# Self-attention's first norm and first projections moved into the adapter's slots

## What is computed

```python
# adapter, L0
hs = _mha(hidden_states @ Wq, enc @ Wk, enc @ Wv)                 # 8 heads of 20
ca_hs1 = _mha(ca_q1[:, indices, :], residual, residual)           # tokens over x
ca_hs2 = _mha(ca_hs1 @ Wq, ca @ Wk_ca, ca @ Wv_ca)                # 4 token keys
x = (hs + ca_hs2) @ Wout + b_out + residual
# block, L1
y = layer_norm(x, g1, be1)
x = cross_attention(y, y, wq1, wk1, wv1, wo1, bo1) + x            # 20 heads of 64
```

## Time and profile before

| | us |
|---|---|
| median of 3 runs | 1039.35 |
| lowest and highest run | 1038.76, 1040.11 |
| the profiled execution | 1038.5 |
| its span | 1036.7 |
| TensorE busy | 981.3 |
| VectorE busy | 690.3 |
| ScalarE busy | 591.5 |
| GpSimd busy | 380.1 |

### The profile page before, as it was taken

How to read it: one execution, slowest core, us unless ns; L and a number is a source line. 1 busy time by engine, 2 the same in 40 slices (tenths; PEclk the granted TensorE clock), 3 DMA queues, 4 the chain that set the end, 5 groups by cost and what they waited for, 6 DMA issues and landing times.

```text
span 1036.7 us, 17534 instructions
## 1 busy us (share of the span) xinstructions
PE 981.3 (95%) x6376; PEld 707.1 (68%) x6376; DVE 690.3 (67%) x1171; ACT 591.5 (57%) x1332; POOL 380.1 (37%) x493
## 2 busy tenths in 40 slices
PE   7999978999999999999999999999989999999998
PEld 4566666666667656667666667666647589999887
DVE  2767646677773776773676773776753889999563
ACT  2666634766763667763667763667753555455442
POOL 2576623434332344342344341343330024444220
PEclk9999999999999999999999999999999999999999
DMA  6400050000000000000000000000000340000000
GB/s 134 94 2 1 1 147 1 1 1 2 1 1 2 1 1 2 1 1 1 2 1 1 1 1 1 2 1 1 2 1 8 101 110 1 1 1 1 2 26 26
DMA packets 25370, 17.64 MB, mean 17 GB/s; under 512 B 8565, under 2 KB 24101, under 8 KB 25285
## 3 DMA queue, kind: packets, MB, share of 16 engines
q1 hardware_dynamic: 25285, 16.52, 6.6%
HBM read 11.26 MB, written 1.31 MB: 12 GB/s over the span
## 4 chain that ended last, share of the span: by engine, by line
PE 64%; DVE 10%; ACT 5%; issue 4%; POOL 1%; DMA 0%; SPq 0%; DVEq 0%; ACTq 0%; POOLq 0%
PE banks L409 13%; PE banks L396 12%; PE banks L382 11%; PE banks L416 4%; ACT sa_probs L499 3%; PE banks L224 3%; PE banks L227 2%; PE banks L226 2%; PE banks L225 2%; PE banks L1641 2%; PE banks L1933 2%; DVE sa_negmax L571 2%; DVE ca_top L1776 2%; DVE ca_probs L1781 1%; PE banks L232 1%
## 5 line engine op out<-in xcount | busy, mean ns | idle before, releaser
L639 POOL TENSOR_SCALAR sa_probs<-sa_probs,sa_inverse 128x512 f32<-128x512 f32 x320 | 217.7, 696 | 372.4 <-DVE sa_inverse L575 372.3
L499 ACT ACTIVATE sa_probs<-banks,sa_negmax 128x512 f32<-128x512 f32 x320 | 215.8, 685 | 163.5 <-DVE sa_negmax L571 163.4
L571 DVE TENSOR_REDUCE sa_negmax<-banks 128x2 f32<-128x1024 f32 x160 | 188.8, 1219 | 12.4 <-PE banks L382 9.7
L396 PEld LDWEIGHTS banks<-ident,sa_probs 128*128 128x128 f32 x1280 | 145.7, 141 | 55.6 <-issue 27.6
L396 PE MATMUL banks<-ident,sa_probs 128*128 128x128 f32 x1280 | 174.0, 277 | 10.0 <-ACT sa_turned L510 5.8
L580 DVE COPY sa_turned<-banks 128x512 f32<-128x512 f32 x160 | 110.2, 689 | 76.3 <-PE banks L396 76.3
L409 PE MATMUL banks<-sa_turned,sa_v 128*64 128x512 f32 x640 | 155.0, 605 | 0.0
L382 PE MATMUL banks<-sa_k_parts,sa_q_parts 64*128 64x512 f32 x960 | 134.9, 412 | 1.9 <-ACT sa_probs L499 1.9
L510 ACT COPY sa_turned<-banks 128x512 f32<-128x512 f32 x160 | 94.3, 590 | 30.6 <-PE banks L396 28.8
L382 PEld LDWEIGHTS banks<-sa_k_parts,sa_q_parts 64*128 64x128 f32 x960 | 85.2, 187 | 31.2 <-issue 14.4
L409 PEld LDWEIGHTS banks<-sa_turned,sa_v 128*64 128x64 f32 x640 | 38.7, 136 | 74.3 <-issue 73.0
(11 more groups left out here) (218 smaller groups left out, 1724.9 us busy)
## 6 DMA issues: line engine op xcount, KB each, us to landing
w_o<-in_L_xattn_wo SPq DMA_DIRECT2D x2, 800.0 KB, 9.2
out<-x SPq DMA_DIRECT2D x4, 320.0 KB, 2.4
w_q_t<-in_L_xattn_wq_t SPq DMA_DIRECT2D x1, 1120.0 KB, 10.4
fold_values<-ca_turned SPq DMA_DIRECT2D x5, 192.5 KB
x<-in_x SPq DMA_DIRECT2D x1, 960.0 KB, 5.8
fold_values<-ca_probs SPq DMA_DIRECT2D x4, 192.5 KB
w_q_t<-in_L_xattn_wq SPq DMA_DIRECT2D x1, 640.0 KB, 6.6
w_o<-in_L_xattn_wk SPq DMA_DIRECT2D x1, 640.0 KB, 10.0
```

Of the source, the lines that this page charges most:

```text
L396: last = pe.transpose(b_turn[e][:, q * P:(q + 1) * P], probs[:, j % 2, e, q, k * P:(k + 1) * P], ident[:])
L499: act.activation(probs[:, j % 2, e, q, :], b_scores[u % 2][:, e, :], ACT.Exp, bias=negmax[:, u % RING, e:e + 1], accum_out=total[:, u % RI ...
L571: dve.tensor_reduce(negmax[:, u % RING, :], b_scores[u % 2], AX_X, ALU.max, negate=True).then_inc(s_max.sem, 1)
L639: pool.tensor_scalar(probs[:, j % 2, e, q, :], probs[:, j % 2, e, q, :], inverse[:, u % RING, e:e + 1], 1.0, ALU.mult, ALU.mult).then_inc( ...
```

## The change

1. The norm's steps move: statistics and deviations from slot 14 to slot 11, standardising from 15 to 13, turning and scaling from 17 to 14 (`NORM_AT`), rounding and remainder from 17 to 15. Its two turned items now take banks of the ring.
2. `project_first` makes q and k of pair 0 at the end of slot 16 and of pair 1 at the end of slot 17, in banks 0 and 1; `round_first` and `rest_first` round them there. Self-attention has these left out, and adds to its semaphores what they would have.
3. To make room: q_parts and k_parts are kept from the adapter on; x_pad has two buffers instead of three; the small weights, context and tokens lie in `turned`; k_all lies in the norm's `hat`; q2 in hs1; wq_ca in probs1.
4. With two buffers x is padded for the next batch in k = 0 (before: two batches ahead in k = 3), and is turned and copied in k = 1 (before k = 0); both groups of queries are projected in k = 3 (before one in k = 1).

```diff
@@ Turns.of_slot
-        if k == 0 and b + 1 < B:
+        if k == 1 and b + 1 < B:
             out += [("x", b + 1, g) for g in range(G)]
-        if k == 1 and b + 1 < B:
-            out += [("queries", b + 1, 0)]
         if k == 2 and 1 <= b <= B:
             out += [("expanded", b - 1, 0)]
+        if s == NORM_AT:
+            out += [("norm", 0, i) for i in range(2)]
...
         if k == 3 and b + 1 < B:
-            out += [("queries", b + 1, 1)]
+            out += [("queries", b + 1, g) for g in range(G)]
@@ adapter, tiles
+        turned = sb("turned", [P, TR, (CH - 1) * P])
+        room = turned[:].rearrange("p r c -> p (r c)")
+        wk, wv, wk_ca, wv_ca = (room[0:CTX, i * HC:(i + 1) * HC].rearrange("p (h c) -> p h c", h=H0) for i in range(4))
...
-        x_pad = sb("x_pad", [P, 3, QT, H0, HP])
+        x_pad = sb("x_pad", [P, 2, QT, H0, HP])
...
-        k_all = sb("k_all", [P, G, B * SK])
+        k_all = next_ln.hat[:].rearrange("p q d -> p (q d)")[:, 0:G * B * SK].rearrange("p (g n) -> p g n", g=G)
@@ adapter, TensorE
+            def project_first(j):
+                if j == 0:
+                    next_ln.ready(pe, 0)
+                    pe.wait_ge(s_exp1.sem, s_exp1.at(NU - 1, 1))
+                    pe.wait_ge(s_rest.sem, s_rest.at(len(chunks) - 1, 1))
+                else:
+                    pe.wait_ge(s_qklo.sem, s_qklo.at(0, 1))
+                for i in range(2):
+                    next_ln.project(pe, banks[i], splits[i][1], j * P).then_inc(s_qk.sem, 1)
...
-                if s == NU + 1:
-                    pe.wait_ge(s_exp1.sem, s_exp1.at(NU - 1, 1))
-                    next_ln.turn(pe, 0, ident, banks[0:2], lambda i: None)
+                if s == NORM_AT:
+                    pair = [("norm", 0, i) for i in range(2)]
+                    next_ln.turn(pe, 0, ident, [ring.bank(banks, item) for item in pair], lambda i: ring.wait_free(pe, pair[i]))
+                    pe.wait_ge(next_ln.s_turned.sem, next_ln.s_turned.at(0, 1))
+                    pe.sem_inc(ring.s_made, 2)
+                if s in (NU, NU + 1):
+                    project_first(s - NU)
@@ adapter, ScalarE
+            def round_first(j):
+                act.wait_ge(s_qk.sem, s_qk.at(j, 0))
+                act.activation(q_parts[:, j, 0, :], banks[0], ACT.Copy, scale=SCALE1).then_inc(s_qkhi.sem, 1)
+                act.wait_ge(s_qk.sem, s_qk.at(j, 1))
+                act.copy(k_parts[:, j, 0, :], banks[1]).then_inc(s_qkhi.sem, 1)
...
-                if s == NU + 1:
+                if s == NORM_AT:
                     act.wait_ge(s_later, 16 * len(later))
-                    next_ln.scale_and_round(act, 0, banks[0:2], lambda eng: None)
+                    next_ln.scale(act, 0, [ring.bank(banks, ("norm", 0, i)) for i in range(2)])
+                    act.wait_ge(next_ln.s_full.sem, next_ln.s_full.at(0, 1))
+                    act.sem_inc(ring.s_act, 2)
+                if s == NORM_AT + 1:
+                    next_ln.round(act, 0, lambda eng: None)
+                if s in (NU, NU + 1):
+                    round_first(s - NU)
@@ adapter, VectorE
-                if k == 0 and b + 1 < B:
+                if k == 1 and b + 1 < B:
                     copy_x(b + 1)
+                if k == 0 and 1 <= b and b + 1 < B:
+                    pad_x(b + 1)
                 if k == 3 and b < B:
                     copy_folded(b)
-                if k == 3 and b + 2 < B:
-                    pad_x(b + 2)
-                if s == NU - 2:
+                if s == NORM_AT - 3:
                     dve.wait_ge(s_x.sem, s_x.at(QT - 1, 0))
                     next_ln.statistics(dve, 0)
-                if s == NU - 1:
+                if s == NORM_AT - 1:
+                    dve.wait_ge(s_kd.sem, s_kd.at(B - 1, 0))
                     next_ln.standardize(dve, 0)
-                if s == NU + 1:
+                if s == NORM_AT + 1:
                     next_ln.remainder(dve, 0, lambda eng: None)
+                if s in (NU, NU + 1):
+                    rest_first(s - NU)
@@ selfattn, TensorE (ScalarE and VectorE likewise)
-            ln.ready(pe, 0)
-            project_q(0, 0, b_proj)
-            project_k(0, 0, b_out)
-            project_q(0, 1, b_turn[0])
-            project_k(0, 1, b_turn[1])
+            for s in (s_q, s_k):
+                pe.sem_inc(s.sem, 2)
             scores(0, 0)
             scores(0, 1)
             project_v(0, 0, b_proj)
-            pe.wait_ge(s_klo.sem, s_klo.at(0, 0))
             project_v(0, 1, b_out)
```

More of the change, by code:

```diff
@@ L510, in copy_turned @@
                 act.copy(turned[:, u % 2, 1, :], b_turn[1]).then_inc(s_evac_act.sem, 1)
-            round_q(0, 0, b_proj)
-            round_k(0, 0, b_out)
-            round_q(0, 1, b_turn[0])
-            round_k(0, 1, b_turn[1])
+            for s in (s_qhi, s_khi):
+                act.sem_inc(s.sem, 2)
             exps(0, 0)
@@ L730, in wait_copied, with adapter @@
         eng.wait_ge(self.copied(item), same.index(item) + 1)
-def adapter(nc, t, x, ident, ctx_t, banks, splits, raws, later, last, next_ln):
+def adapter(nc, t, x, ident, ctx_t, banks, splits, raws, later, last, next_ln, q_parts, k_parts):
     w = lambda n: t["L0_xattn_" + n]
@@ L1069, in _ @@
                     scores2(b - 1)
-                if k == 1 and b + 1 < B:
-                    project_queries(b + 1, 0)
                 if k == 2 and 1 <= b <= B:
```

65 lines of the change are left out of this document (34 added, 31 removed).

## The result

| | before | after |
|---|---|---|
| median, us | 1039.05 (1038.34 to 1040.11, 4 runs) | 1047.99 (1046.08 to 1048.37, 4 runs) |
| profiled execution, us | 1038.5 | 1047.87 |
| its span, us | 1036.7 | 1046.1 |
| its mean granted clock | 0.993 | 0.987 |

The ratio is 1.0085, 95% interval 1.0072 to 1.0098: slower by 8.9 us, where the forecast was 1040.9 and its range ended at 1043.4.

The account below looks back on a forecast made before the run. TensorE, busy 95%, bounds the kernel, with VectorE setting the pace in token-softmax slots. Terms -5.9 +1.65 +1.2 +1.0 +4.9 -1.3 = +1.55 us on 1038.5 give 1040.05, as median 1040.9; 8-in-10 range 1035.6 to 1043.4.

Parts of the forecast that it names:

- Border: From the adapter's last update of x to self-attention's first maxima: 2.4 us instead of 8.3, a gain of 5.9 us.
- Slots 0 to 11: Adapter slots 0 to 11: moved x turning and query projections make slot 12 start some 3.85 us later.
- Slots absorb the moves: Rival: TensorE bounds slots 1 to 10, so moves there cost 0.5 instead of 3.85; 1035.65 us in all; chance 0.28.
- Slots 13 and 14: Adapter slots 13 and 14: standardising delays the token softmax, the norm's turning waits for ScalarE's copy; +4.9 us.
- Slots 16 to 18: From the end of the token products to the adapter's last update: 18.2 us instead of 19.5, -1.3 us.
- Sum at full clock: Whole kernel: the terms sum to +1.55 us, the border gain given only if the clock is full.
- The clock falls in slot 14 and at the border: Rival: the clock halves once in slot 15 and again behind the border, 2.35 us more, 1043.25 us; chance 0.19.
- Part 6: Slots 16 to 19: projections added, four output projections at full clock take 5.5 us instead of 7.1; -1.3 us in all.
- part 1: Border of adapter and self-attention: projections leave, first scores take some 0.85 us; gain 5.9 us if the clock is full.
- the rule: GpSimd contends with VectorE over SBUF, so standardising in slot 13 takes long; otherwise the total is -0.9 instead of +1.55 us.
- part 5: Slots 13 and 14: standardising beside POOL takes 2.4 us and TensorE waits; +4.9 us, bounds 1.1 and 6.5.

Follow-up runs that it names:

- no_proj: The changed kernel with the four projections, their roundings and remainders back at the start of self-attention; 1046.35 us, ratio 1.0066.
- fill_all: As fill14, with unread transposes also around the last expansion in slot 18, at the adapter's end and at the border; 1043.14 us, ratio 1.0048.
- fill14: The changed kernel with 28 unread transposes of the identity where TensorE waits in slot 14; 1042.64 us, ratio 1.0041.
- before_fill: The kernel before with unread transposes ahead of the last expansion, at the adapter's end and ahead of the first projections; 1035.79 us, ratio 0.9968.
- best_fill: best with unread transposes in slots 13 and 14 and at the border; 1037.47 us, ratio 0.998.
- best_late_fill: best_late with 7 unread transposes in slot 14 and 14 at the border; 1033.59 us, ratio 0.995.
- best: The change with old slot order, norm two slots earlier, second pair's projections in slot 18, first pair's k rounding behind the copy TensorE needs; 1037.51 us.
- best_late: best with the norm's remainders in slot 15 behind the folded values and slot 14's copy of expanded probabilities first; 1032.09 us, ratio 0.9929.

## Why the prediction was wrong

The terms, by its own parts:

- *Border, 5.9 us.* Measured 5.3 in the change and by no_proj; the maxima come 3.03 us behind the update, since the meeting takes longer (scores start 1.83 us behind the update's end, and in the profile after six of them run at half clock). Near right.
- *Slots 0 to 11, +3.85.* Measured +3.84 after, +3.3 at full clock, and 0 with the old order. "Slots absorb the moves" is refuted. That the sum fits to 0.01 us is luck: slots 0 to 3 cost 2.31 (1.65 foretold), of which about half a microsecond is the half clock of slot 2, slots 4 to 7 cost 0.56 (1.2), and only slots 8 to 11 are right, 0.97 (1.0).
- *Slots 13 and 14, +4.9.* Measured +5.86, +5.44 filled. Both waits came where they were foretold (1.8 and 2.0; they were 2.18 and 1.63). The standardising took 3.23 us, not 2.4.
- *Slots 16 to 18, -1.3.* Measured -0.5 at full clock. Its own parts gave -1.0: 10.8, 1.9 and 5.5 us end with TensorE's last product, the 19.5 us before with the update of x 0.37 us behind it. The sum hid two large opposed terms, which no_proj separates: -3.6 from the early norm (-5.1 with the clock) and +4.65 from the projections.
- *Sum at full clock.* +1.55 predicted, which counts the removal of the two half-clock places before as a gain; fill_all's profile is 3.5 us longer than before's up to the first product with the values (2.9 in all), with what its fillers cost in it. So the terms were 1.9 us too low: 0.5 in slots 12 to 14, 0.8 in slots 16 to 18 and 1.3 at the border, less 0.7 elsewhere.

**The step that failed is the rival "The clock falls in slot 14 and at the border"**, with its price of 2.35 us, its chance of 0.19 and the sentence "Against it: both waits are shorter than the one that brought it before." The clock did fall, behind waits of 2.18 and 1.63 us, behind 1.34 and 0.87 us in slot 18, and even behind 0.88 and 0.59 us in slot 2:

```profile
31.07 0.52 PE L914 MATMUL banks<-ident,ad_probs 96*128 96x96 f32 x4 [0.88 <-ACT ad_x_t L1137]
32.18 0.52 PE L914 MATMUL banks<-ident,ad_probs 96*128 96x96 f32 x4 [0.59 <-DVE ad_x_t L1240]
32.54 1.93 PE L982 MATMUL banks<-ad_k_diag,ad_q_t 128*128 128x292 f32 x4
```

(L982 takes 1.15 us at full clock.) The five stretches, against none in fill_all, cost 6.2 us, counted stage by stage, and not 2.35: 2.3 us in slots 15 and 16 (1.5 foretold), 2.0 for the two places behind the border (0.85 foretold, for one), and, with no price at all in the rival, 1.6 in slot 18 and some 0.5 in slot 2; what fill_all's own fillers cost at the border goes off. So 6.2 of the 8.1 us that the profiles lie above the sum are this step, and 1.9 the terms above. Part 6 then counted "four output projections at full clock" and part 1 had the condition "if the clock is full": the first output projection took 2.47 us again, exactly as before, and the first scores 2.44 instead of 1.65. The range ended at the centre of that rival, though it named two places of several where it could happen; it should have reached past the 1046 of its own highest bounds.

**Where the rule bore.** The four standardising instructions took 0.81 us each in slot 13 (0.64 before, 0.30 in self-attention). The first, begun before GpSimd's scaling at 123.63, took 0.35 us; the other three end at 124.94, 125.76 and 126.69, each 0.10 us behind a GpSimd instruction (the scaling and the two weight remainders, which end at 124.84, 125.66 and 126.59). What part 5 had too small is this pairing. It fits VectorE waiting for GpSimd; no run took GpSimd's work away. What the Trainium skill, page "GPSIMD Engine Reference", section "Key points", says of contention between GpSimd and VectorE agrees in direction; no run here shows which interface it is.

**What stays open.** Where TensorE's standing still was filled, the clock behind it was full in the profiles of fill14, fill_all and before_fill, and all three are faster in the median than without fillers; best_fill and best_late_fill are not. The same waits do not always bring the half clock. Slot 18 of fill14 has the change's very waits (1.34 and 0.87 us) and a clock of 1.00 behind them; best and best_late wait 0.95 and 0.94 us at the same place of slot 13, and the clock fell in best alone (0.72 in 114 to 120). What else decides was not found, and no run isolated it. The clock's mean goes with the spread of one program's runs, up to 7.7 us, and may be why the effects of half changes did not add.

## What to carry to other kernels

Price each new wait of TensorE twice: for its own length, and for the half clock that may follow it, also where the wait is 1 or 2 us; with several such places the upper end of the range must hold them all. A move that takes work out of a border pays only if it lands in a wait that stays one: the pair's projections in slot 17 gave back nearly all they won, in slot 18 they cost 1.5 us (15.9 us from the token products to the last update in best, 14.4 in no_proj). And look at which instruction stands directly ahead of the short serial chain (here the token softmax): the standardising, placed there, brought TensorE a wait of 2.18 us, and the remainders in the same place one of 2.21 us.

## What was unexpected of the hardware

Transposes that nobody reads made the kernel before 0.3% faster (interval 0.2 to 0.4%). The remainder of the norm's tail, 32 partitions of 512, took 1.92 us in slot 15 and 1.24 us in slot 13, against 0.68 us at its old place in slot 17, where GpSimd stood still; the remainder of 128 partitions took 0.95, 1.56 and 0.69 us in the same slots. Such a price goes not with the size but with what GpSimd does beside it: in best_late the tail's remainder ends at 138.66, 0.56 us behind GpSimd's addition of the bias (136.12 to 138.10), and in best the two remainders end 0.55 us behind GpSimd's scaling (124.39) and its weight remainder (125.66).
